# The fifth passes of two context products placed in 64 rows each, with the steps of an attention pipeline rearranged around them

## The chip, the cores and the metric

The kernel runs on one core of one Trainium2 chip. The metric is the device time of the whole kernel in microseconds (us). A difference under 0.2% of it, some 3 us, can't be told from no change.

## What is computed

```python
B, LQ, C = 32, 112, 256;  LKV, CTX = 375, 192;  H, DK = 16, 64      # for each of 32 batches:
q = layernorm(x) @ Wq;  k, v = split(ctx @ Wkv)                      # K = 192 rows of context
atten = softmax(q @ k.T * DK ** -0.5);  x = x + (atten @ v) @ Wproj + bproj
h = layernorm(x);  probs = softmax(h @ gate_w)                       # then 8 experts, the best 2 per token
x = x + sum over the 2 experts of share * (silu(h @ Wg) * (h @ Wu)) @ Wd
```

All in float32 accuracy. TensorE's products are made of parts: a matrix is split into a high part (`fp32r`) and a low rest, and high x high, high x low and low x high are added up in one bank.

## The kernel before

**Two stages.** From 35 us to about 1233 us of the profiled execution the attention of the 32 batches runs; then the rows are gathered per expert and 63 expert tiles follow. The change is in the first stage alone.

**A batch is four steps.** `pair(i)` does batches 2i (`odd` = 0) and 2i + 1, each in steps s = 0 to 3 of four heads. On TensorE (PE) a step is: scores of four heads into banks 0 to 3 (L1191); transposes of the softmaxed rows, `turn_prob`, two heads and then two (L1201); `weigh`, probabilities x V (L1220). Between them stand the products made ahead for the next batch: 8 products K (376 columns), 6 products V (512 columns), q (6 passes of 224 columns), xT. Which one stands where is the table `ahead(odd, s)` in three parts, `first`, `second`, `third`; all use banks 4 and 5 in turn (`Ahead.bank`, `bank_before`), and each waits until the bank's last content was copied out. In some steps stand also `turn_inverses` (step 1 and 3), `project` (step 0, the batch before), `turn_hn` (2), `gate_logits` (3) and `count` (1); these share bank 7 (`C_ps`).

**Row groups.** A head has 64 rows, so the score passes of two heads stand in rows 0 to 63 and 64 to 127 of the array and are issued as a pair. A context product (`product_ctx`, L1161) has 192 rows to sum over: passes 1 to 3 are the parts of the first 128; the other 64, the tail, take passes 4 and 5. Pass 4 multiplies the tail's weight `WkT` (the same 64 rows twice) by `yB`, whose upper 64 rows are the high part of the context and whose lower 64 its low part. Pass 5 multiplies the low part `WkU` by `yB`, 128 rows too.

**The other engines.** VectorE (DVE): the four row maxima of the scores (L973), the low parts of K and q (`low_part`, L851), two of four copies of transposed probabilities (L979), `normalise` (L903), `residual` (L911 to L918), routing (`choose`, `mark`, `assign`). ScalarE (ACT): the exponentials (L730), the high parts and V out of their banks (`evacuate`, L689 to L695), the other two copies (L736). GpSimd (POOL): the parts of the context (`split_y`), of the attention output (`split_O`), the norms and scatters. Each engine takes its instructions in the written order; semaphores carry all order between engines.

Of the kernel before, what the change touches and what calls it, by code (L numbers as in the profile page):

```python
# [32 lines left out]
P = 128  # L33
# [28 lines left out]

def ahead(odd, s):


    first = [("K", 2 * s), ("V", ((0, 2), (1, 0), (1, 2))[s]) if s < 3 else ("K", 7)]
    if odd:
        second = [("K", 2 * s + 1), ("q", s)] if s < 3 else [("q", s)]
    else:
        second = [("K", 2 * s + 1), ("q", HALF + s)] if s < 3 else [("xT", 0)]  # L70
    third = {0: [], 1: [("V", (1, 1))], 2: [("V", (0, 0))], 3: [("V", (0, 1))]}[s]
    if not odd:
        third = {2: [("q", 7)], 3: [("xT", 1)]}.get(s, []) + third
    return [(odd, s, part, kind, a) for part, items in enumerate((first, second, third)) for kind, a in items]


PAIR = [it for odd in (0, 1) for s in range(NS) for it in ahead(odd, s)]
assert len(PAIR) % 2 == 0 and [it[3] for it in PAIR[-2:]] == ["q", "V"]
START = [(1, -1, 0, kind, a) for kind, a in (
    ("K", 0), ("xT", 0), ("xT", 1), ("K", 1), ("K", 2), ("K", 3), ("q", 0), ("q", 1),  # L80
    ("K", 4), ("K", 5), ("q", 2), ("K", 6), ("K", 7), ("V", (0, 0)), ("q", 3), ("V", (0, 1)))]
START_BANKS = [k % 6 for k in range(len(START) - 2)] + [0, 1]
assert len(START) % 2 == 0
LAST = [it for it in PAIR if it[3] != "xT" and not (it[0] and (it[3] in "Kq" or it[4] in ((0, 0), (0, 1))))]


def n_split(items):
    return sum(it[3] != "V" for it in items)


class Ahead:


    def __init__(self, i):
# [3 lines left out]
        self.first = i is None  # L98
        self.n0 = base * len(START) + k * len(PAIR)
        self.split0 = base * n_split(START) + k * n_split(PAIR)  # L100
        self.v0 = base * (len(START) - n_split(START)) + k * (len(PAIR) - n_split(PAIR))
        self.bank0 = base * len(START) % 2

    def at(self, odd, step):

        return [[k for k, it in enumerate(self.items) if it[:3] == (odd, step, part)] for part in range(3)]
# [4 lines left out]
    def bank(self, k):  # L111
        return START_BANKS[k] if self.first else (self.bank0 + k) % 2

# [7 lines left out]
    def split(self, k):  # L121
        return self.split0 + n_split(self.items[:k + 1])
# [1284 lines left out]
```

## Time and profile before

| | us |
|---|---|
| median of 3 runs (1604.51 to 1605.93) | 1604.6 |
| profiled execution, its own time | 1601.43 |
| its span, first to last instruction | 1599.6 |
| PE busy / DVE busy / ACT busy | 1539.4 / 921.8 / 810.6 |

The granted clock of the core is 0.99 over the span. Rows of the profile name engine, line, operation and tile; `x12` is a count, `[0.58 <- ...]` idle time of the engine before the row and what ended it. A matmul's row lasts longer than its distance to the next one, since matmuls overlap: what one costs is read from the starts of neighbouring rows.

### The profile page before, as it was taken

The numbers are of one execution on the slowest core, as the hardware profiler recorded it, in microseconds if no ns is written. First come the engines' busy times: TensorE is split into PE (matmuls) and PEld (weight loads), VectorE is DVE, ScalarE is ACT, GpSimd is POOL, SyncE is SP. The second block draws the span as 40 slices with busy tenths as digits, with TensorE's granted clock in tenths as the row PEclk, the third lists the DMA queues.
The fourth block names the chain that finished last, engine by engine and source line by source line (L and its number), as shares of the span: only waits on it lengthen the run. The fifth ranks groups of instructions, "written<-read, shape, count | busy, mean of one in ns | idle before, by whom it ended". The sixth has DMA issues, their size and how long they took to land.

```text
span 1599.6 us, 37516 instructions
## 1 busy us (share of the span) xinstructions
PE 1539.4 (96%) x12134; PEld 1357.0 (85%) x12135; DVE 921.8 (58%) x2483; ACT 810.6 (51%) x2187; POOL 543.9 (34%) x603
## 2 busy tenths in 40 slices
PE   5999999999999999999999999999998599999997
PEld 4888888898889888898889888988887488888886
DVE  5566666666666666666666666666666633333332
ACT  4555555555556556555555555655554322222221
POOL 4224233433333233323342433333235223322332
PEclk9999999999999999999999999999999799999999
DMA  6411112111111112211111111112014333333332
GB/s 162 115 52 49 55 48 59 48 53 48 53 48 53 48 58 61 72 56 48 56 48 53 50 57 48 53 48 82 12 46 174 110 53 50 49 52 53 49 49 30
DMA packets 82704, 96.19 MB, mean 60 GB/s; under 512 B 6912, under 2 KB 77808, under 8 KB 82672
## 3 DMA queue, kind: packets, MB, share of 16 engines
q1 hardware_dynamic: 68960, 74.67, 16.1%
q0 software_dynamic: 12144, 15.66, 6.0%
q10 hardware_dynamic: 1568, 5.44, 1.0%
q8 instruction: 19, 0.31, 0.1%
q14 instruction: 13, 0.11, 0.0%
HBM read 44.85 MB, written 50.90 MB: 60 GB/s over the span
## 4 chain that ended last, share of the span: by engine, by line
PE 91%; DVE 3%; DMA 2%; ACT 2%; issue 2%; SPq 0%; POOLq 0%; DVEq 0%; ACTq 0%
PE bank L1161 30%; PE bank L1107 21%; PE bank L1220 10%; PE bank L1191 9%; PE bank L1201 9%; PE bank L1380 7%; PE bank L1364 2%; PE bank L1229 2%; PE bank L1324 1%; DMA WqL_whole<-in_L_xattn_Wq 1%; DVE probT L979 1%; PE bank L1270 1%; ACT K_h L691 1%; ACT prob L730 1%; DMA Wgu<-in_L_ffn_gate_up_w 0%
## 5 line engine op out<-in xcount | busy, mean ns | idle before, releaser
L730 ACT ACTIVATE prob<-bank,neg_max 112x375 f32<-112x375 f32 x512 | 295.0, 579 | 351.0 <-DVE neg_max L973 351.0
L973 DVE TENSOR_REDUCE neg_max<-bank 112x1 f32<-112x375 f32 x512 | 244.5, 540 | 77.5 <-PE bank L1191 75.6
L1201 PE MATMUL bank<-ident,prob 112*125 112x112 f32 x1536 | 212.7, 273 | 3.1 <-ACT prob L730 3.1
L1201 PEld LDWEIGHTS bank<-ident,prob 112*125 112x125 f32 x1536 | 198.7, 188 | 16.4 <-ACT prob L730 5.6
L851 DVE TENSOR_TENSOR K_l<-bank,K_h 128x376 fp32r<-128x376 f32 x256 | 140.2, 549 | 105.2 <-ACT K_h L691 104.4
L671 POOL DMA_INDIRECT out<-y_out,dest_now x63 | 97.8, 1552 | 244.4 <-ACT y_out L819 219.0
L1107 PE MATMUL bank<-Wgu,hT_h 128*128 x504 | 175.3, 429 | 2.7 <-DVE hT_l L1064 2.7
L1220 PE MATMUL bank<-probT,V 125*64 125x112 f32 x3072 | 175.5, 263 | 0.0
L596 POOL CAST OT_h<-O_now 128x448 fp32r<-128x448 f32 x64 | 35.7, 558 | 376.6 <-DVE O_now L903 376.6
L1220 PEld LDWEIGHTS bank<-probT,V 125*64 125x64 f32 x3072 | 148.0, 137 | 18.2 <-issue 0.4
L689 ACT COPY V<-bank 125x512 f32<-125x512 f32 x192 | 112.6, 586 | 93.8 <-PE bank L1161 89.4
L1085 DVE COPY hidT<-bank 128x512 f32<-128x512 f32 x63 | 43.5, 691 | 173.8 <-PE bank L1364 173.8
L691 ACT CAST K_h<-bank 128x376 fp32r<-128x376 f32 x256 | 120.6, 472 | 38.2 <-PE bank L1161 35.0
L979 DVE COPY probT<-bank 125x336 f32<-125x336 f32 x256 | 117.9, 501 | 31.8 <-PE bank L1201 31.7
L1161 PE MATMUL bank<-yA_h,WkH 128*128 128x376 f32 x256 | 109.5, 428 | 14.3 <-DVE WkU L869 14.3
L819 ACT ACTIVATE y_out<-bank,share_now 128x256 f32<-128x256 f32 x63 | 29.9, 475 | 179.3 <-PE bank L1380 179.3
L1380 PE MATMUL bank<-Wd,hidT 128*128 x504 | 119.1, 379 | 0.9 <-DVE hidT L1085 0.9
L1380 PEld LDWEIGHTS bank<-Wd,hidT 128*128 128x128 f32 x504 | 95.4, 189 | 16.4 <-issue 1.1
L903 DVE TENSOR_TENSOR O_now<-bank,inv_rows 128x448 f32<-128x448 f32 x64 | 40.0, 624 | 115.5 <-PE bank L1220 110.6
L1107 PEld LDWEIGHTS bank<-Wgu,hT_h 128*128 128x128 f32 x504 | 90.9, 191 | 18.1 <-issue 3.6
L730 ACT ACTIVATION_READ_ACCUMULATOR prob<-bank,neg_max 112x1 f32 x512 | 103.7, 203 | 0.0
L736 ACT COPY probT<-bank 125x336 f32<-125x336 f32 x256 | 101.5, 444 | 1.1 <-PE bank L1201 0.2
(163 smaller groups left out, 3676.5 us busy)
## 6 DMA issues: line engine op xcount, KB each, us to landing
bins<-pad_rows SPq DMA_DIRECT2D x29, 1032.0 KB, 6.2
h_in<-bins SPq DMA_DIRECT2D x63, 129.0 KB, 2.1
y_sb<-in_ctx SPq DMA_DIRECT2D x32, 187.5 KB, 2.4
y_sb<-in_ctx SPq DMA_DIRECT2D x62, 93.8 KB, 2.5
Wgu<-in_L_ffn_gate_up_w SPq DMA_DIRECT2D x4, 1024.0 KB, 5.0
Wgu<-in_L_ffn_gate_up_w ACTq DMA_DIRECT2D x4, 1024.0 KB, 9.8
x_sb<-in_x SPq DMA_DIRECT2D x16, 224.0 KB, 2.9
x_res<-in_x SPq DMA_DIRECT2D x32, 112.0 KB, 5.6
```

What stands on the lines that cost most here:

```text
L689: nc.scalar.copy(V[:, t, half * 512:half * 512 + 512], src[0:KR, :]).then_inc(v_done, 1)
L691: nc.scalar.copy(K_h[:, arg, :], src[:, 0:LKE]).then_inc(hi_done, 1)
L730: nc.scalar.activation(prob[:, j, :], S_ps[j][0:LQ, 0:LKV], ACT.Exp, bias=neg_max[:, j:j + 1], accum_out=row_sum[:, head // HB, head % HB: ...
L851: nc.vector.tensor_tensor(lo, ps, hi.bitcast(F32), ALU.subtract).then_inc(lo_done, 1)
L973: nc.vector.tensor_reduce(neg_max[:, j:j + 1], S_ps[j][0:LQ, 0:LKV], AX.X, ALU.max, negate=True).then_inc(max_done, 1)
L979: nc.vector.tensor_copy(probT[:, j, :], S_ps[j][0:KR, 0:KT * LQ]).then_inc(probT_first, 1)
L1107: last = mm(dst, w, m, start=n == 0, stop=n == len(todo) - 1)
L1161: last = mm(dst, w if weights_stay else y, y if weights_stay else w, start=n == 0, stop=n == len(todo) - 1)
L1191: last = mm(S_ps[2 * k + r][0:LQ, 0:LKE], w[rows, p, q], m[rows, p, :], start=n == 0, stop=n == len(todo) - 1)
L1201: last = nc.tensor.transpose(S_ps[j][0:KR, t * LQ:t * LQ + LQ], prob[:, j, t * KR:t * KR + KR], ident[0:LQ, 0:LQ])
L1220: last = mm(O_ps[r * DK:r * DK + DK, c:c + LQ], V[:, t, (2 * p + r) * DK:(2 * p + r) * DK + DK], probT[:, 2 * k + r, t * LQ:t * LQ + LQ], ...
L1380: last = mm(down_ps[(k + 1) % 2][:, 0:C], hidT[:, j, :], Wd[:, experts[k], j, :], start=j == 0, stop=j == FJ - 1)
```

## The change

1. Pass 5 of a context product now takes 64 rows, from a new tile `yT` (the tail's high part in both halves of the rows), and the fifth passes of two products are issued as a pair in the two row groups (`tails`). For the two K products of a step they come first, right behind the scores; for the two V products last, right behind `weigh` and ahead of the next step's scores. The start of the kernel keeps five passes.
2. Each step makes both its K products directly one after the other, and 2 V products in steps 0, 1 and 3 (none in 2). K and V use banks 4 and 5; q and xT use bank 7 except in step 2.
3. One V of each pair of V products is copied out by DVE (`SECOND`), the other by ACT as before.
4. The small work moves: `project` from step 0 to step 2, with `normalise` and `residual` accordingly; `turn_hn` to step 3; `gate_logits`, `choose`, `mark`, `count`, `assign` later too. DVE does the maxima first in each step.
5. POOL makes `yT` (one more cast per batch) and splits the context earlier in its order.
6. The start makes one more q and two more V products; the last batch makes two V fewer.

```diff
+    q_at = {(1, 0): (0,), (1, 1): (1,), (1, 2): (2, 3), (1, 3): (4,), (0, 0): (5,), (0, 1): (6,), (0, 2): (7,)}.get((odd, s), ())
+    one = [("q", p) for p in q_at] + {(0, 2): [("xT", 0)], (0, 3): [("xT", 1)]}.get((odd, s), [])
+    places = {"K": [("K", 2 * s), ("K", 2 * s + 1)],
+              "early": one if s < 2 else [],
+              "mid": one[:1] if s >= 2 else [],
+              "V": [("V", t) for t in {0: ((1, 1), (1, 2)), 1: ((0, 0), (0, 1)), 3: ((0, 2), (1, 0))}.get(s, ())],
+              "late": one[1:] if s >= 2 else []}
+SECOND = ((1, 2), (0, 1), (1, 0))
...
+                pool.tensor_copy(yT[:, slot, 0:LKV], y_sb[:, slot, 1, :]).then_inc(yT_done, 1)
...
+                    if arg in SECOND:
+                        dve.wait_ge(made, a.made(k))
+                        nc.vector.tensor_copy(V[:, t, half * 512:half * 512 + 512], src[0:KR, :]).then_inc(v_second, 1)
...
+            def tails(a, two, begin):
+
+                for r, k in enumerate(two):
+                    out, w, y = context_operands(a, k, 3, slice(r * CT, r * CT + CT))
+                    last = mm(out, w, y, start=begin, stop=not begin)
+                    if not begin:
+                        last.then_inc(made, 1)
...
                         if there(b, B):
                             scores(a, odd, s, b)
-                        for k in first[:1]:
+                        if of_K:
...
+                            for k in of_K:
+                                free_bank(a, k)
+                            tails(a, of_K, True)
+                            for k in of_K:
+                                context_product(a, k, False, True).then_inc(made, 1)
...
+                        if s == 2 and there(b - 1, B):
...
+                            project(b - 1)
                         if s == 3 and there(b - 1, B):
-                            gate_logits(b - 1)
...
+                            turn_hn(b - 1, 1 - odd)
                         if there(b, B):
                             turn_prob(b, s, 0)
-                        for k in second:
+                        for k in of_V[:1]:
+                            free_bank(a, k)
+                            context_product(a, k, True, False)
...
                         if there(b, B):
                             weigh(a, odd, s, b)
+                        if of_V:
+                            tails(a, of_V, False)
```

On PE, the end of step 0 and the start of step 1 before the change (`bank<-probT,V` is `weigh`, `K_h,q_h` and the like are scores, `yA_h,WkH` is pass 1 of a K product):

```order
L1220 MATMUL bank<-probT,V 64x112 [waits probT_first,v_done]
L1220 MATMUL bank<-probT,V 64x112 x5
L1220 MATMUL bank<-probT,V 64x112 [waits probT_second]
L1220 MATMUL bank<-probT,V 64x112 x5
L1191 MATMUL bank<-K_h,q_h 112x376 [waits lo_done]
L1191 MATMUL bank<-K_h,q_h 112x376
L1191 MATMUL bank<-K_l,q_h 112x376 x2
L1191 MATMUL bank<-K_h,q_l 112x376 x2
L1191 MATMUL bank<-K_h,q_h 112x376 x2
L1191 MATMUL bank<-K_l,q_h 112x376 x2
L1191 MATMUL bank<-K_h,q_l 112x376 x2
L1161 MATMUL bank<-yA_h,WkH 128x376 [waits lo_done]
```

The same place after it (L1281 is `weigh`, L1247 scores, L1219 `tails`, L1212 passes 1 to 4):

```order
L1281 MATMUL bank<-probT,V 64x112 x5
L1219 MATMUL bank<-WvU,yT 125x512 x2
L1247 MATMUL bank<-K_h,q_h 112x376 x2
L1247 MATMUL bank<-K_l,q_h 112x376 x2
L1247 MATMUL bank<-K_h,q_l 112x376 x2
L1247 MATMUL bank<-K_h,q_h 112x376 x2
L1247 MATMUL bank<-K_l,q_h 112x376 x2
L1247 MATMUL bank<-K_h,q_l 112x376 x2
L1219 MATMUL bank<-yT,WkU 128x376 [waits v_second,v_done]
L1219 MATMUL bank<-yT,WkU 128x376
L1212 MATMUL bank<-yA_h,WkH 128x376
L1212 MATMUL bank<-yA_l,WkH 128x376
```

The pair of V passes stands ahead of the scores and the pair of K passes behind them; the K pair waits for both copies of V out of banks 4 and 5, which nothing waited for at this place before.

On DVE, the end of step 1 and the start of step 2 after the change (L885 is the copy of V, L1017 the maxima, L895 the low parts of K, L947 `normalise`, L955 to L962 `residual`):

```order
L885 COPY V<-bank 125x512 [waits made]
L1016 REGISTER_ALU
L1017 TENSOR_REDUCE neg_max<-bank 112x1 [waits scores_made]
L1016 REGISTER_ALU
L1017 TENSOR_REDUCE neg_max<-bank 112x1 [waits scores_made]
```

The copy of V is new on this engine and stands ahead of all four maxima. Further on in step 2:

```order
L895 TENSOR_TENSOR K_l<-bank,K_h 128x376 [waits hi_done]
L944 ISA [waits inv_out]
L947 TENSOR_TENSOR O_now<-bank,inv_rows 128x448 [waits OT_lo,pv_made]
L954 REGISTER_ALU [waits xb_done,proj_made]
L955 TENSOR_TENSOR x_103<-bank,x_bias 112x256 [waits x2_out1]
L957 BN_STATS stat_106<-x_103 112x6 [waits x2_done]
L962 BN_AGGR mv_107<-stat_106 112x2 [waits st2,hn_twin]
L1023 COPY probT<-bank 125x336 [waits probT_made] x2
```

Before, `residual` stood ahead of the maxima of step 1:

```order
L911 TENSOR_TENSOR x_103<-bank,x_bias 112x256 [waits x2_out1]
L913 BN_STATS stat_106<-x_103 112x6 [waits x2_done]
L918 BN_AGGR mv_107<-stat_106 112x2 [waits st2,hn_twin]
L972 REGISTER_ALU
L973 TENSOR_REDUCE neg_max<-bank 112x1 [waits scores_made]
```

So `residual` now stands behind the maxima, and it is the copies of the transposed probabilities of step 2 that have it, and with it the wait for `project`, ahead of them.

## Rows read from the trace of the kernel before

**Rows 1.** The profile's first line: the span.
```profile
span 1599.6 us, 37516 instructions
```

**Rows 2.** Busy time by engine in one stretch: PE, PEld, DVE, ACT, POOL, granted clock, DMA.
```profile
500.00:1000.00 500.00, 497.42 (x4345) 444.71 (x4344) 319.81 (x892) 290.47 (x824) 175.00 (x215) 1.00 0.18 53
```

**Rows 3.** PE's waits in the whole span: us in total, times, longest.
```profile
PE bank L1161 <- DVE xT_l L851: 5.5, 15, 0.4
...
PE bank L1161 <- DVE WvU L869: 3.9, 1, 3.9
```

**Rows 4.** The chain that ended last, in order of time: start, us, what.
```profile
504.95 1.21 PE bank L1191 x12
...
529.80 2.81 PE bank L1107 x24
...
580.40 1.21 PE bank L1191 x12
```

**Rows 5.** Timeline of PE around the scores of one step: start, us, instruction.
```profile
505.66 0.33 PE L1191 MATMUL bank<-K_l,q_h 64*112 64x376 f32 x2
...
505.83 0.33 PE L1191 MATMUL bank<-K_h,q_l 64*112 64x376 f32 x2
...
506.09 0.44 PE L1161 MATMUL bank<-yA_h,WkH 128*128 128x376 f32 x1
...
506.37 0.33 PE L1161 MATMUL bank<-yA_l,WkH 128*128 128x376 f32 x1
...
506.54 0.33 PE L1161 MATMUL bank<-yA_h,WkL 128*128 128x376 f32 x1
```

**Rows 6.** The same step further on: V passes, transposes, the second K product.
```profile
507.98 0.39 PE L1161 MATMUL bank<-WvU,yB 128*125 128x512 f32 x1
...
508.21 0.81 PE L1201 MATMUL bank<-ident,prob 112*125 112x112 f32 x6
...
508.78 0.42 PE L1161 MATMUL bank<-yA_h,WkH 128*128 128x376 f32 x1
...
509.04 0.33 PE L1161 MATMUL bank<-yA_l,WkH 128*128 128x376 f32 x1
```

**Rows 7.** Timeline of PE in step 3 of the even batch.
```profile
519.71 0.35 PE L1129 MATMUL bank<-ident,xn 112*128 112x112 f32 x2
...
520.44 0.50 PE L1161 MATMUL bank<-WvH,yA_h 128*125 128x512 f32 x1 [0.37 <-DVE xT_l L851]
```

**Rows 8.** Timeline of DVE and ACT, step 3 (its first score pass starts at 514.56).
```profile
514.56 0.42 PE L1191 MATMUL bank<-K_h,q_h 64*112 64x376 f32 x2
...
515.36 1.91 DVE L973 TENSOR_REDUCE neg_max<-bank 112x1 f32<-112x375 f32 x4 [1.60 <-PE bank L1191]
...
515.95 0.57 ACT L730 ACTIVATE prob<-bank,neg_max 112x375 f32<-112x375 f32 x1 [2.19 <-DVE neg_max L973]
...
517.06 0.47 ACT L691 CAST K_h<-bank 128x376 fp32r<-128x376 f32 x1
```

**Rows 9.** Costliest groups: instructions by which DVE empties banks; mean ns of one.
```profile
L851 DVE TENSOR_TENSOR K_l<-bank,K_h 128x376 fp32r<-128x376 f32 x256 | 140.2, 549 | 105.2 <-ACT K_h L691 104.4
...
L1085 DVE COPY hidT<-bank 128x512 f32<-128x512 f32 x63 | 43.5, 691 | 173.8 <-PE bank L1364 173.8
...
L979 DVE COPY probT<-bank 125x336 f32<-125x336 f32 x256 | 117.9, 501 | 31.8 <-PE bank L1201 31.7
```

**Rows 10.** Timeline of DVE: `norm_x`; first and last of `mark`'s eight; `residual`.
```profile
511.27 0.74 DVE L832 BATCH_NORM_STATS2 stat<-x_sb 112x6 f32<-112x256 f32 x2
...
529.88 0.16 DVE L939 CAST top_f<-top_i 112x2 f32<-112x2 uint32 x1
...
530.57 0.16 DVE L954 TENSOR_SCALAR dest<-dest 112x2 f32<-112x2 f32 x1
...
532.65 0.42 DVE L911 TENSOR_TENSOR x<-bank,x_bias 112x256 f32<-112x256 f32 x1 [1.92 <-PE bank L1107]
...
533.72 0.18 DVE L918 BATCH_NORM_AGGREGATE mv<-stat 112x2 f32<-112x6 f32 x1 [0.18 <-DVE stat L913]
```

More of the change, by code:

```diff
@@ L55 @@
 W = C + 2
+PLACES = ("K", "early", "mid", "V", "late")
 def ahead(odd, s):
[L66 to L73, printed above, removed]
@@ new lines, with evacuated_as, how_many, bank_of @@
+LAST = [it for it in PAIR if it[3] != "xT" and not (it[0] and (it[3] in "Kq" or it[4] not in NOW))]
+def evacuated_as(it):
+    return "split" if it[3] != "V" else "values_y" if it[4] in SECOND else "values_x"
+def how_many(items, kind):
+    return sum(evacuated_as(it) == kind for it in items)
+def bank_of(items, k):
+    if items is START:
+        return START_BANKS[k]
+    odd, s, place, kind, a = items[k]
+    if kind == "K":
+        return a % 2
+    if kind == "V":
+        return int(a in SECOND)
+    return 7 if s != 2 else int(place == "late")
@@ L1007, in pair @@
                             turned(b, s, 1)
-                        if s == 1 and there(b - 2, B):
-                            assign(b - 2, odd)
-                        for k in second:
+                        for k in made_at["early"] + made_at["mid"]:
                             low_part(a, k)
@@ L1145, in make @@
                 else:
[L1146 to L1149 removed]
+                    assert a.first
+                    if kind == "V":
                         pe.wait_ge(w_lo, 5)
[L1151 to L1153 removed]
@@ L1155, in product_ctx @@
[L1155 to L1163 removed]
+                    elif arg == 0:
+                        pe.wait_ge(y_lo, 1)
+                        pe.wait_ge(yB_lo, 1)
@@ new lines, in make, with context_operands @@
+                    context_product(a, k, True, False)
+                    out, w, y = context_operands(a, k, 3)
+                    last = mm(out, w, y, start=False, stop=True)
+                last.then_inc(made, 1)
+            def context_operands(a, k, n, rows=slice(0, P)):
+                odd, step, place, kind, arg = a.items[k]
+                bank = START_ps[a.bank(k)]
+                slot = odd if kind == "V" and arg in NOW else 1 - odd
+                high, low, tail, tail_low = (WkH, WkL, WkT, WkU) if kind == "K" else (WvH, WvL, WvT, WvU)
+                w = {0: high, 1: high, 2: low, "both": tail, 3: tail_low}[n]
+                y = {0: yA_h, 1: yA_l, 2: yA_h, "both": yB, 3: yB if a.first else yT}[n]
+                if kind == "K":
+                    return bank[:, 0:LKE], w[rows, arg * P:arg * P + P], y[rows, slot, 0:LKE]
+                half, t = arg
+                return bank[0:KR, :], y[rows, slot, t * KR:t * KR + KR], w[rows, half * 512:half * 512 + 512]
@@ new lines, in context_product @@
+            def context_product(a, k, begins, ends):
+                for n in (0, 1, 2, "both"):
+                    out, w, y = context_operands(a, k, n)
+                    last = mm(out, w, y, start=begins and n == 0, stop=ends and n == "both")
+                return last
+            def tails(a, two, begin):
[4 more added lines that the diff above has]
+                        last.then_inc(made, 1)
```

297 lines of the change are left out of this document (162 added, 135 removed).

## Prediction

> **What bounds the kernel now.** I read the page first, then busy time by stretch, PE's waits, the chain in order of time, and the timeline of one pair of batches on every engine. The span is 1599.6 us [rows 1]; the time is counted from the profiled execution's own 1601.43 us, which lies 3.2 under the median of 1604.6, and that is added back at the end. In the steady part PE is busy 497.4 of 500 us while DVE has 320 and ACT 290 [rows 2]. A busy PE may still be one that waits inside overlapped rows, so the waits count more: over the whole span PE has one recurring wait, for the low part of xT, 15 times (once per pair of batches), and one of 3.9 us at the start for the low part of the V weights [rows 3]. In the chain the reader is to see the period: the scores that open a pair of batches start at 504.95 and again at 580.40, so **75.45 us per pair** [rows 4]. The kernel is bound by the number of passes that PE issues; what PE saves is saved in full, as long as no other engine becomes late.
>
> **What a pass costs.** It is the distance between two starts. Two score passes in the two row groups together take 0.17 us (505.66 to 505.83), and a full K pass of the same 376 columns takes 0.17 too (506.37 to 506.54) [rows 5]. A V pass of 512 columns takes 0.23 (507.98 to 508.21) [rows 6]. A change of kind costs about 0.09 more: from the last scores to the first K pass 0.26 (505.83 to 506.09) [rows 5], and the first fp32r pass behind transposes 0.26 (508.78 to 509.04) [rows 6].
>
> **The change, per pair of batches (16 K, 12 V products).**
> 1. *Fifth passes.* Now 16 x 0.17 + 12 x 0.23 = 5.5 us. As 8 + 6 pairs: for K the score pairs are the same operation in the same row groups with the same columns, so a pair takes 0.17. No pair of 512 columns is in the trace; it lies between one V pass, 0.23, and two, 0.46. I take 0.23, since the score pair shows no surcharge over one pass. Saving 8 x 0.17 + 6 x 0.23 = **2.74**; with V pairs at 0.46 it is 1.4, with both kinds unoverlapped 0.
> 2. *Both K products in a row.* The second K product has stood behind transposes; behind the first its first pass loses the 0.09: 8 x 0.09 = **0.7** saved. The V products all come behind transposes or small work; 4 of 12 stand directly behind a K product now and one behind q: 5 x 0.09 = **0.45** lost. `project`, 24 passes in 2.81 us [rows 4], no longer follows transposes: 0.2 saved. The tails need no change of kind of their own: the one from `weigh` to the scores is now paid by the V pair, the one from the scores to K by the K pair.
> 3. *xT.* Its two transposes take 0.73 us until the V product behind them starts (519.71 to 520.44), of which 0.37 is a wait for DVE's low part that has to free the bank [rows 7]; two transposes by themselves take 0.57 / 6 x 2 = 0.2 [rows 6]. In the new order no product in the same bank follows: **0.5** saved.
> 4. *Evacuation.* Six copies of V go to DVE. The nearest row, also 512 columns out of a bank, takes 0.69 us [rows 9]. POOL's extra cast hides in its idle 65% [rows 2].
>
> Sum on PE: 2.74 + 0.7 - 0.45 + 0.2 + 0.5 = 3.7 us per pair, if nothing waits.
>
> **What could be late.** The new waits are at two places.
> *K pair.* It follows the scores, 6 x 0.17 = 1.03 us after the step's start, and waits until both copies of V are out. The V pair ends about 0.17 after that start (starts 0.23 ahead, a V row lasts 0.39 [rows 6]). DVE's copy then runs from about 0.2 to 0.9, ACT's is no longer. Slack 0.1. Behind it on DVE are the maxima; they start 0.8 after the first score (514.56 to 515.36) [rows 8] since the scores are not there before. So the copy costs them at most 0.1. Queued behind the K pair on PE is everything of the step.
> *Transposes.* The first exponential starts 1.39 after the first score (514.56 to 515.95), two take 1.11, and the copy of K's high part 0.47 [rows 8]; it comes between them now. The second exponential, with its copy of K at 2.4 to 2.85 (K's first four passes end at 2.35), ends at about 3.4. PE reaches the first transposes of that head at 1.03 + 0.26 + 8 x 0.17 + 0.1 + `turn_hn` 0.3 + half the transposes 0.3 = 3.4 in step 3, later elsewhere: a tie. In steps 0 and 1 a q product stands ahead.
> *Step 2.* `project` starts 2.8 after the first score and takes 2.8: its result is there at 5.8. DVE's `residual` takes 532.65 to 533.90 = 1.25 [rows 10], then two copies of probabilities, 0.50 each [rows 9], together until 8.0. PE is at `weigh` at about 7.9 in the even batch (transposes, q, transposes, xT) and at 8.4 in the odd one, which has two q. It waits 0.1 to 0.2 once per pair.
> *DVE's fullest step* is step 1 of the even batch: V 0.69, maxima 1.91 [rows 8], two low parts of K 1.10, two copies 1.0, low q up to 0.55 [rows 9], `mark` 0.85, `norm_x` 0.74 and two aggregates of 0.18 [rows 10]: 7.2. The inverses and `choose`, seven instructions of 0.16 to 0.5 like the rows there, I put at 1.2. That is 8.4 in a step of some 8.8. It fits, barely. On the mean DVE goes from 320 of 500, 6.0 per step, to 6.5 per step of 9.0.
> I take 0.2 per pair for all of these: **3.5 us per pair**, new period 71.9.
>
> The Trainium skill bears on this twice. "TensorEngine Tiling (Array Packing)", section PSUM Bottleneck, says that packing speeds up TensorE but not the emptying of PSUM, which may then become the bottleneck. By that rule the time would go to rival B or D below instead of to the sum; with DVE at 320 of 500 us [rows 2] the trace leaves it room. "TensorE: Matmul & The Clock Gate", Part 3 (the cost: per-tile semaphore tail), gives 26 ns for every further increment of a semaphore by a tile. The V pairs carry one increment on each of their two passes; as an estimate by that page's figure this would add 6 x 0.026 = 0.16 us per pair of batches, 2.4 us in all. No row of before has such a pair of 512 columns.
>
> **Sum.** Pairs 0 to 14: 15 x 3.5 = 52.5. Batch 30: 4 x 0.17 + 3 x 0.23 + 4 x 0.09 = 1.7, and a q product (6 passes of 0.117, 2.81 / 24 [rows 4]) less: 2.4. Batch 31 makes two V products less, 2 x 1.2 = 2.4 of PE work, but without work to make ahead it is not bound by PE: I take 1 of it. The start makes those three products more; q fits in the 3.9 us wait [rows 3], two V products do not: 0 to 2.4 lost, I take 0.5, since the start also loses a q from among its V products. The end behind the last `weigh` keeps its chain. Together 55.4. 1601.43 - 55.4 = 1546.0, with the 3.2 of the median **1549**.
>
> **Rivals.**
> A. *As above*, at most 0.3 us more or less per pair: 1544 to 1555. Chance 0.64.
> B. *Partly given back to waits.* Speaks for it: the tie before the first transposes, slack of 0.1 at the K pair, 8.4 of 8.8 on DVE. Against: each is computed without a loss. If every step loses 0.15 us, 1.2 per pair, 15.5 pairs lose 18.6: 1568. Range 1555 to 1580. Chance 0.20.
> C. *Row-group pairs don't overlap for the context.* The score pairs speak against it. Without the 2.74: 15.5 x 2.74 = 42.5 less, 1591; with the V pairs alone at 0.46, 1.38 x 15.5 = 21 less: 1570. Chance 0.06.
> D. *Slower: DVE's copy of V comes late in all six steps that have one.* PE stands at the K pair with both row groups empty, while the maxima behind the copy are late too, so that the step shifts whole. It decides when the copies are late by more than 3.5 / 6 = 0.6 us each beyond the slack; 1 us late costs 6 - 3.5 = 2.5 per pair: 1604.6 + 15.5 x 2.5 = 1643. DVE's load of 73% and its written order, with nothing long between `assign` or `mark` and the copy except in one step, speak against. Chance 0.04.
> E. *More than that.* Batch 31 gains its full 2.4 and more, since the first steps of the last batch have less on PE, and waits hidden inside PE's overlapped rows go: 1537 to 1544. Chance 0.06.
>
> **Numbers.** A, E and the lower part of B with the lower part of C up to 1570 hold 0.8 and some: 1540 to 1571. Faster by over 0.2% (3.2 us, what a measurement can tell): all but D and a remnant of C, 0.95; within 0.2%: 0.01; slower: 0.04.
>
> **What would show it.** The chain should show the opening scores 71.5 to 72.3 us apart. The timeline: V pairs 0.23 to 0.25 and K pairs 0.17 apart from their neighbours, the second K product's first pass at 0.17, no wait for xT. PE's waits: a short one for DVE's `probT` in step 2 of even batches. If V pairs take 0.46, C; if PE waits for V, `v_second`, at the K pair or for `prob` at the transposes in every step, B or D. Wrong would also be a pass that got longer because two row groups read different tiles.

## The result, and the profile after

The changed kernel takes **1568.87 us** (median of 4 runs, 1568.5 to 1570.76) against 1604.82 before: ratio 0.9777, interval 0.976 to 0.9794. It is 36 us faster, where 55 were forecast: faster as predicted and inside the range of 1540 to 1571, but 20 us above the number and 14 above the range of the main forecast A (1544 to 1555), where rival B had been put (1568).

The first lines of the page of after, to be read beside [rows 1] and the table of before:

```profile
span 1566.4 us, 37570 instructions
...
PE 1503.0 (96%) x12134; PEld 1321.0 (84%) x12135; DVE 968.7 (62%) x2579; ACT 762.3 (49%) x2091; POOL 555.2 (35%) x636
```

The same 500 us as in [rows 2], busy time of PE, PEld, DVE, ACT and POOL:

```profile
500.00:1000.00 500.00, 499.71 (x4513) 444.84 (x4510) 350.81 (x963) 281.15 (x813) 182.36 (x234) 1.00 0.19 56
```

PE is now busy for all but 0.3 of the 500 us, and that row says nothing of waits: a matmul whose weights are loaded late overlaps the one before and hides the gap. So starts were compared. Where the span's 33.2 us come from, by the starts of the scores that open a pair of batches, the end of the last `weigh` and the start of the first expert tile in both traces:

| stretch | gain forecast | gain measured |
|---|---|---|
| start, until the first scores (35.79, after 38.97) | -0.5 | -3.2 |
| pairs 0 to 14 (period 75.45, after 72.63; first pair 71.95, after 70.25) | 52.5 | 41.3 |
| last two batches (68.7, after 68.8) | 3.4 | -0.1 |
| end of the last `weigh` until the experts (25.0, after 29.8) | 0 | -4.8 |

The span's miss is 22 of 55.4 (in the medians 20, since the profiled execution of before lay 3.2 under its median). Every term was too high, and the period accounts for only half of it. The timeline of after around the start of step 0 of an odd batch, and the same place one period later (start, us, instruction); it answers to [rows 5]:

```profile
507.96 0.49 PE L1219 MATMUL bank<-WvU,yT 64*125 64x512 f32 x2
...
508.29 0.33 PE L1247 MATMUL bank<-K_h,q_h 64*112 64x376 f32 x2
...
508.52 0.69 DVE L885 COPY V<-bank 125x512 f32<-125x512 f32 x1 [1.87 <-PE bank L1219]
...
509.14 0.33 PE L1247 MATMUL bank<-K_h,q_l 64*112 64x376 f32 x2
509.33 0.21 PEld L1219 LDWEIGHTS bank<-yT,WkU 64*128 64x128 f32 x2 [0.18 <-issue]
509.36 0.44 PE L1219 MATMUL bank<-yT,WkU 64*128 64x376 f32 x2
...
509.73 0.44 PE L1212 MATMUL bank<-yA_h,WkH 128*128 128x376 f32 x1
...
580.92 0.33 PE L1247 MATMUL bank<-K_h,q_h 64*112 64x376 f32 x2
```

The V pair costs 0.33 until the scores (508.29 - 507.96): 0.23 and a change of kind of 0.10, both as forecast. The last scores start at 509.14, so the K pair could start at 509.31 and its weights load ahead of it. They load at 509.33, just after DVE's copy of V has ended (508.52 + 0.69 = 509.21). The pair then needs 0.37 (509.36 to 509.73) until the first K pass. Step 3, where no V pair stands ahead and no copy has to be waited for:

```profile
536.70 0.19 PEld L1219 LDWEIGHTS bank<-yT,WkU 64*128 64x128 f32 x2
...
536.86 0.33 PE L1219 MATMUL bank<-yT,WkU 64*128 64x376 f32 x2
...
537.12 0.44 PE L1212 MATMUL bank<-yA_h,WkH 128*128 128x376 f32 x1
...
538.12 0.47 ACT L727 CAST K_h<-bank 128x376 fp32r<-128x376 f32 x1 [0.33 <-PE bank L1212]
...
538.49 0.58 ACT L767 ACTIVATE prob<-bank,neg_max 112x375 f32<-112x375 f32 x1
...
538.80 0.99 PE L1257 MATMUL bank<-ident,prob 112*125 112x112 f32 x6
...
539.56 0.48 PE L1212 MATMUL bank<-WvH,yA_h 128*125 128x512 f32 x1
```

Here the weights are loaded 0.16 ahead and pair to K pass is 0.26. So the late release would cost 0.15 per step (0.11 behind the pair, 0.04 ahead of it), six times per pair of batches; experiment 2 tests it. And the transposes (538.80) take 0.76 until the V pass, since the second exponential, behind the copy of K, ends at 539.07: six need 0.57 by [rows 6].

PE's waits in the whole span, to be read beside [rows 3]:

```profile
PE bank L1155 <- POOL OT_l L624: 7.2, 1, 7.2
PE bank L1155 <- DVE K_l L895: 4.0, 1, 4.0
...
PE bank L1290 <- DVE inv_wide L938: 2.4, 3, 1.6
PE bank L1257 <- ACT prob L767: 2.4, 3, 0.9
...
PE bank L1281 <- DVE probT L1023: 1.1, 2, 0.9
```

The 15 waits for xT are gone, as forecast. The rows that are left stand at three places: the start (K_l), the last two batches (inv_wide, prob, probT) and behind the last `weigh` (OT_l).

### The profile page after: what moved, and what is told of

The parts are those of the page before. It is cut to its first block and busy times, and to the rows that moved or that the text cites. A ratio compares the mean times of both kernels' runs of the same rounds, so it can differ in the third digit from the quotient of the medians.

```text
span 1566.4 us, 37570 instructions
## 1 busy us (share of the span) xinstructions
PE 1503.0 (96%) x12134; PEld 1321.0 (84%) x12135; DVE 968.7 (62%) x2579; ACT 762.3 (49%) x2091; POOL 555.2 (35%) x636
## 3 DMA queue, kind: packets, MB, share of 16 engines
q10 hardware_dynamic: 1568, 5.44, 1.0%
## 5 line engine op out<-in xcount | busy, mean ns | idle before, releaser
L1017 DVE TENSOR_REDUCE neg_max<-bank 112x1 f32<-112x375 f32 x512 | 243.9, 539 | 19.4 <-PE bank L1247 19.3
L895 DVE TENSOR_TENSOR K_l<-bank,K_h 128x376 fp32r<-128x376 f32 x256 | 140.4, 550 | 64.9 <-ACT K_h L727 62.4
L1281 PE MATMUL bank<-probT,V 125*64 125x112 f32 x3072 | 176.6, 264 | 2.0 <-DVE probT L1023 1.1
L1281 PEld LDWEIGHTS bank<-probT,V 125*64 125x64 f32 x3072 | 149.1, 137 | 14.6 <-issue 2.6
L885 DVE COPY V<-bank 125x512 f32<-125x512 f32 x96 | 66.4, 692 | 151.3 <-PE bank L1219 147.4
L725 ACT COPY V<-bank 125x512 f32<-125x512 f32 x96 | 56.4, 587 | 119.2 <-PE bank L1219 115.9
L1212 PE MATMUL bank<-yA_h,WkH 128*128 128x376 f32 x256 | 99.1, 387 | 14.5 <-DVE WkU L913 14.5
L673 POOL TENSOR_SCALAR std<-mv 112x1 f32<-112x1 f32 x32 | 7.7, 241 | 293.6 <-DVE mv L962 293.6
L767 ACT ACTIVATION_READ_ACCUMULATOR prob<-bank,neg_max 112x1 f32 x512 | 107.5, 210 | 0.0
```

Source lines behind the costliest of these rows:

```text
L767: nc.scalar.activation(prob[:, j, :], S_ps[j][0:LQ, 0:LKV], ACT.Exp, bias=neg_max[:, j:j + 1], accum_out=row_sum[:, head // HB, head % HB: ...
L895: nc.vector.tensor_tensor(lo, ps, hi.bitcast(F32), ALU.subtract).then_inc(lo_done, 1)
L1017: nc.vector.tensor_reduce(neg_max[:, j:j + 1], S_ps[j][0:LQ, 0:LKV], AX.X, ALU.max, negate=True).then_inc(max_done, 1)
L1212: last = mm(out, w, y, start=begins and n == 0, stop=ends and n == "both")
L1281: last = mm(O_ps[r * DK:r * DK + DK, c:c + LQ], V[:, t, (2 * p + r) * DK:(2 * p + r) * DK + DK], probT[:, 2 * k + r, t * LQ:t * LQ + LQ], ...
```

## Experiments

All diffs are against the changed kernel.

### 1. The pairing alone undone: `e1_single_tails`

```diff
-                y = {0: yA_h, 1: yA_l, 2: yA_h, "both": yB, 3: yB if a.first else yT}[n]
+                y = {0: yA_h, 1: yA_l, 2: yA_h, "both": yB, 3: yB}[n]
...
-                    out, w, y = context_operands(a, k, 3, slice(r * CT, r * CT + CT))
+                    out, w, y = context_operands(a, k, 3)
```

> The changed kernel with every fifth pass as before, alone in 128 rows, at its new place; all else stays rearranged. If a pair of passes in two row groups costs one pass, the period per pair of batches grows from 72.63 us by 8 x 0.17 + 6 x 0.23 = 2.74 to about 75.4, back to the 75.45 of before, and the time to about 1568.9 + 15.5 x 2.74 = 1611: the rearrangement alone would then be worth nothing in the steady part and lose at both ends. Rival: the pairs overlap only in part for 512 columns; then the period grows by 1.4 to 2 us, to 74.0 to 74.6.

Measured: 1613.72 (ratio to before 1.006, 1.0043 to 1.0077), period 75.6. The pairing is worth 2.97 per pair of batches; 2.74 was forecast. The other half of the result: the rearrangement by itself is no gain in the steady part (75.6 against 75.45). This run is 9.2 us slower than before (1604.54 beside it); its 15 pairs account for 3.5 of that by the starts, the rest lies in the ends.

### 2. Short copies of V: `e2_short_copies`

From the second pair of batches on both engines copy only 128 of the 512 columns of V, so three quarters of the later V are left out. On ACT, and alike on DVE:

```diff
-                    nc.scalar.copy(V[:, t, half * 512:half * 512 + 512], src[0:KR, :]).then_inc(v_done, 1)
+                    n = 512 if a.first or a.previous is START else 128
+                    nc.scalar.copy(V[:, t, half * 512:half * 512 + n], src[0:KR, 0:n]).then_inc(v_done, 1)
```

> The copies of V out of their banks take 128 of 512 columns from the second pair of batches on (the output is then wrong), so that both banks are free some 0.4 us earlier. Theory, late release: the K pair behind the scores starts late and without its weights loaded ahead since DVE's copy ends at 0.92 us of the step; then the distance from the K pair to the first K pass falls from 0.37 to 0.26 and that from the first scores to the pair from 1.07 to 1.03, six times, and the period from 72.63 to about 71.7, the time by some 13 us to 1555. Rival, fixed price: a pair whose weight load stands behind semaphore waits always costs this; then the period stays at 72.6.

Measured: 1558.14 (ratio 0.9716, 0.97 to 0.9732), period 71.7 to 71.95, against the expected 71.7 and 1555. The timeline of PE and of the copies at the same place:

```profile
504.92 0.33 PE L1249 MATMUL bank<-K_h,q_h 64*112 64x376 f32 x2
...
505.15 0.29 DVE L887 COPY V<-bank 125x128 f32<-125x128 f32 x1 [1.87 <-PE bank L1221]
...
505.95 0.34 PE L1221 MATMUL bank<-yT,WkU 64*128 64x376 f32 x2
506.21 0.44 PE L1214 MATMUL bank<-yA_h,WkH 128*128 128x376 f32 x1
...
576.70 0.33 PE L1249 MATMUL bank<-K_h,q_h 64*112 64x376 f32 x2
```

Scores to K pair is 1.03 instead of 1.07, K pair to K pass 0.26 instead of 0.37, as in step 3. What ended early is the copy; with the copy ending 0.5 ahead of the pair (505.44) instead of 0.1, both fall away. This is shown: the late release costs 0.8 per pair of batches, where six times 0.15 had been expected; the rival, a fixed price, would have left the period at 72.6.

### 3. Both exponentials ahead of both copies of K: `e5_two_exps_first`

```diff
                         if there(b, B):
                             weights_of(b, s, 0)
-                        for k in of_K[:1]:
-                            evacuate(a, k)
-                        if there(b, B):
                             weights_of(b, s, 1)
-                        for k in of_K[1:]:
+                        for k in of_K:
                             evacuate(a, k)
```

> ScalarE does the exponentials of the first two heads of a step before it copies the first K product, instead of one. Theory: in step 3 PE waits 0.18 us in the first transposes for the second exponential, which stands behind that copy and behind ScalarE's wait for the K product; the transposes of step 3 fall from 0.76 to 0.58, the period by 0.36 to 72.3, the time by 5.5 us to 1563. Rival: the copy of K is then 0.13 us later, VectorE's low part too, and the first V product waits for its bank instead: period 72.6.

Measured: 1563.92 (ratio 0.9747, 0.9731 to 0.9764), where 1563 was expected, most periods 72.23. PE in step 3:

```profile
538.37 0.36 PE L1314 MATMUL bank<-ident,hn 112*128 112x112 f32 x2
538.57 0.82 PE L1254 MATMUL bank<-ident,prob 112*125 112x112 f32 x6
539.15 0.48 PE L1209 MATMUL bank<-WvH,yA_h 128*125 128x512 f32 x1
```

The transposes take 0.58 again instead of 0.76. The wait for the second exponential is shown, 0.4 per pair with what follows from it, and the later copies of K cost nothing.

### 4. The V pair ahead of `weigh` in step 0: `e6_tails_first_s0`

```diff
+                        if of_V and s == 0:
+                            tails(a, of_V, False)
                         if there(b, B):
                             weigh(a, odd, s, b)
-                        if of_V:
+                        if of_V and s > 0:
                             tails(a, of_V, False)
```

> In step 0 alone the pair of V passes stands ahead of the weighing instead of behind it, so that V is copied out 1.3 us earlier; steps 1 and 3 stay. Late release: the K pair of step 1 costs 0.15 less, but the order transposes, V pair, weighing, scores has one change of kind more, 0.09 or more: per pair of batches 2 x (0.09 - 0.15), between 72.5 and 72.7. Fixed price: 2 x 0.09 more, 72.8.

Measured: 1570.16 (ratio 0.9787, 0.9771 to 0.9804), period 72.7 to 72.9. In step 1 the K pair no longer waits (pair to K pass 0.27), but there is a change of kind more: 0.43 from the V pair to `weigh`, where a V pass costs 0.23, and 0.26 instead of 0.17 from the first scores to the next. The period lies where the fixed price had been expected (72.8), not where the late release was (72.5 to 72.7): the release is no longer late, as the 0.27 shows, but the further change cost 0.20 and not the 0.09 that was taken. Moving the wait away this way costs what it saves.

### 5. GpSimd's split of expert 2 at another place: `e3a_expert2_early`, `e3b_expert2_last`

In POOL's order of the last batch it stands behind the norm that waits for `residual`, a `split_O` and a scatter. `residual` is two steps later now, and so the split starts at 1194.21, when the last `weigh` has begun (1193.50); before the change it started 11.6 us ahead of that `weigh` (1219.96 against 1231.54). Early:

```diff
                     if known(i) and i == NP - 1 and odd:
                         split_expert(1)
+                        split_expert(2)
...
-                    if known(i) and i == NP - 1 and odd:
-                        split_expert(2)
```

In the other it stands behind the last `split_O` instead.

> GpSimd splits expert 2 right behind expert 1 in the last batch, not behind the scatter of batch 29. Theory, queue: from the end of the last weighing to the first gathered row on PE it takes 29.8 us in the changed kernel and 25.0 before, since GpSimd's split of expert 2 (6.5 us, 1194.2 to 1200.7) stands ahead of the last split of the attention output, for which project waits 7.2 us. With it gone project starts 2.8 us behind the last weighing as before: 25 us. But GpSimd's long operation would now run under steps 1 and 2 of the last batch, where small VectorE operations have been stretched to its end: the last batch may take up to 4 us more than its 31.4. Total 1564 to 1568. Rival, the routing of batch 30 on VectorE sets the end, not GpSimd: no change of the 29.8.

> GpSimd splits expert 2 behind the last split of the attention output. Queue theory: project starts 2.8 us behind the last weighing; residual of batch 31 stands on VectorE behind the low part of expert 3, which waits for expert 2 (ready some 8.5 us behind the last weighing, plus 2.3), so that residual starts some 11 us behind it, against 12.3 in the changed kernel and 7.4 before: gain 1 to 2 us, 28 to 29 us in place of 29.8, time 1567.5. Rival: no change.

Measured: 1565.3 (ratio 0.9762, 0.9745 to 0.9778) and 1569.92 (0.9789, 0.9772 to 0.9805). The end of the last batch in the changed kernel, and the granted clock while `project` runs:

```profile
1193.50 1.37 PE L1281 MATMUL bank<-probT,V 125*64 125x112 f32 x24
1194.21 1.91 POOL L610 CAST Wgu<-Wgu 128x2048 fp32r<-128x2048 f32 x1
...
1196.21 4.50 POOL L604 TENSOR_TENSOR Wgu<-Wgu 128x2048 fp32r<-128x2048 f32 x1
1196.71 4.02 DVE L983 CAST top_f<-top_i 112x2 f32<-112x2 uint32 x1
...
1201.29 1.14 POOL L624 TENSOR_TENSOR OT_l<-O_now,OT_h 128x448 fp32r<-128x448 f32 x1
...
1202.57 0.53 PE L1155 MATMUL bank<-WpH,OT_h 128*112 128x256 f32 x1 [7.21 <-POOL OT_l L624]
...
1207.13 0.42 DVE L955 TENSOR_TENSOR x<-bank,x_bias 112x256 f32<-112x256 f32 x1 [2.35 <-PE bank L1155]
```

```profile
1202.00:1206.00 4.00, 3.43 (x17) 3.46 (x18) 2.78 (x4) 1.90 (x1) 0.43 (x1) 0.52 1.05 401
```

And with expert 2 early:

```profile
1198.25 0.34 PE L1154 MATMUL bank<-WpH,OT_h 128*112 128x256 f32 x1 [2.35 <-POOL OT_l L624]
...
1201.34 0.42 DVE L954 TENSOR_TENSOR x<-bank,x_bias 112x256 f32<-112x256 f32 x1
```

The last attention output waits behind 6.4 us of GpSimd's work; PE waits 7.2, and the clock is down to 0.52 (1.2 GHz) behind the wait, so that `project` itself takes 4.5 instead of 3.1. With the split early the wait is 2.35, the clock 1.00, and the end of the last `weigh` to the experts takes 23.5 instead of 29.8 (25 was expected). Before the change the wait there was 2.8, and `project` took 4.4 at a low clock too:

```profile
1236.00:1239.00 3.00, 3.00 (x17) 3.00 (x16) 2.11 (x1) 0.00 (x0) 0.00 (x0) 0.51 1.02 404
```

So of the 4.8 that the change lost in the tail, 4.4 are the longer wait (7.2 against 2.8), by one displaced instruction pair; the 1.4 of `project` come on top in the run with the split early. Its profiled execution was also the fastest of its four (1562.63); in the medians the gain is 3.6. With the split behind the last `split_O`, `project` no longer waits for it (2.35 again), but VectorE's last `residual` comes late and PE waits 6.2 for it: 29.0, and a total of 1569.92 against the expected 1567.5.

### 6. The fifth q later in the start: `e4_q4_later`

```diff
-    ("K", 6), ("K", 7), ("q", 3), ("q", 4), ("V", (0, 0)), ("V", (0, 1)), ("V", (0, 2)), ("V", (1, 0)))]
-START_BANKS = [k % 6 for k in range(len(START) - 4)] + [6, 7, 0, 1]
+    ("K", 6), ("K", 7), ("q", 3), ("V", (0, 0)), ("V", (0, 1)), ("q", 4), ("V", (0, 2)), ("V", (1, 0)))]
+START_BANKS = [k % 6 for k in range(len(START) - 5)] + [6, 7, 2, 0, 1]
```

> At the start the fifth q product stands behind two V products and not ahead of all of them. Theory: it waited 4.0 us for VectorE's low part of a K product, queued behind both low parts of the V weights, and held up the V products that were ready at 31.5 us; now the first V pass starts at 31.6 in place of 33.4 and the first scores at about 37 in place of 38.97: 2 us, 1567. Rival: V products wait for their own banks and copies and the first scores stay near 39.

Measured: 1568.95 (ratio 0.9785, 0.9768 to 0.9801), first scores at 38.45. The expected 2 us did not come: V now starts at 31.39, having waited 3.57 for the low part of WvU, and runs at a granted clock of 0.62. What was taken for the cause, q's place in the list, was only the first of two products behind the same late instruction. That led to the instruction itself, experiment 7.

This run's trace shows one thing more. Batch 31, the last, took 27.5 us here and 30.1 in the changed kernel, with the same instructions and the same kinds of wait. The granted clock differs. The row of 1175 to 1182, step 1 of that batch, of the changed kernel and of this run:

```profile
1175.00:1182.00 7.00, 6.39 (x44) 5.12 (x45) 3.33 (x16) 1.85 (x5) 0.81 (x1) 0.51 0.01 2
```

```profile
1175.00:1182.00 7.00, 6.21 (x66) 5.53 (x66) 4.81 (x19) 3.74 (x11) 0.94 (x1) 1.00 0.01 4
```

Before the change the clock was 1.00 over the whole batch. So 2.6 us of the changed kernel's last batch went with a clock at 1.2 GHz in the one execution that was profiled. What decides whether it falls there is not shown: PE had waited 0.94 us twice in the 12 us before, in this run as well, where it did not fall.

### 7. GpSimd's long operation behind VectorE's: `e8_wpl_later`

DVE and POOL at the start of the changed kernel:

```profile
24.58 1.45 DVE L913 TENSOR_TENSOR WvL<-WvL_whole,WvH 128x1024 fp32r<-128x1024 f32 x1 [0.57 <-ACT WvH L716]
25.96 5.56 DVE L913 TENSOR_TENSOR WvU<-WvU_whole,WvT 128x1024 fp32r<-128x1024 f32 x1
...
31.44 0.99 DVE L895 TENSOR_TENSOR K_l<-bank,K_h 128x376 fp32r<-128x376 f32 x2
```

```profile
25.03 5.40 POOL L649 TENSOR_TENSOR WpL<-WpL_whole,WpH 128x2048 fp32r<-128x2048 f32 x1
```

Two alike instructions take 1.45 and 5.56. The long one ends at 31.52, 1.09 after GpSimd's (30.43).

```diff
             pool.wait_ge(wp_done, 1)
+            pool.wait_ge(w_lo, 5)
             pool.tensor_tensor(wp_lo, wp[:].rearrange("p k n -> p (k n)"), wp_hi.bitcast(F32), ALU.subtract).then_inc(wp_done, 1)
```

> The changed kernel with one wait more: GpSimd makes the low part of the projection's weights (128x2048, 5.4 us, from 25.03 to 30.43 in the changed kernel) only when VectorE has made the low parts of the V weights. Theory S (VectorE's operations between two tiles in SBUF cannot run beside a long one of GpSimd): the low part of WvU, 5.56 us from 25.96 to 31.52 in the changed kernel, takes 1.2 to 1.5 like that of WvL ahead of it (1.45), and is done at 27.3; the low part of K behind it comes 4.2 earlier, q no longer waits 4.0, V products start at about 29.3 instead of 33.45 and the first scores at 34.8 to 35.5 instead of 38.97. Time 1565 (1564 to 1566) against 1568.9. Rival T (the 5.56 us are VectorE's own, by its operands, or come from ACT's casts at the same time): WvU still takes over 5 us and nothing moves, 1568 to 1570. Rival U (it takes 1.3, but the start then waits for something else, as in the run with q later): first scores 37 to 38.5, time 1567 to 1568.5.

Measured: 1562.59 (ratio 0.9746, 0.9729 to 0.9762). Its DVE and POOL:

```profile
25.73 1.21 DVE L914 TENSOR_TENSOR WvU<-WvU_whole,WvT 128x1024 fp32r<-128x1024 f32 x1
...
27.10 4.62 POOL L650 TENSOR_TENSOR WpL<-WpL_whole,WpH 128x2048 fp32r<-128x2048 f32 x1 [2.37 <-DVE WvU L914]
```

WvU takes 1.21, GpSimd's own operation 4.62 instead of 5.40, and the first scores come at 33.03 instead of 38.97. That is 5.9 earlier, more than the 4.35 that WvU lost (5.56 - 1.21): without its wait PE also keeps the clock. The row of a window over the V products, changed kernel and this one:

```profile
33.00:35.00 2.00, 2.00 (x8) 1.70 (x7) 1.33 (x4) 0.35 (x1) 0.00 (x0) 0.50 0.03 8
```

```profile
29.00:32.00 3.00, 3.00 (x15) 2.40 (x13) 1.36 (x4) 0.62 (x2) 2.72 (x1) 1.00 0.02 5
```

Theory S stands, with more than it expected (first scores 34.8 to 35.5, time 1564 to 1566). It goes further than the change: the 3.9 us wait of before for WvU's low part [rows 3] has the same form, there with WvL at 5.10 beside GpSimd's 4.59; that it has the same cause was not tested.

### 8. Expert 0's split out of the way of `inv_wide`: `e12_expert0_early`

In the last but one batch the changed kernel has

```profile
1158.51 2.64 DVE L938 COPY inv_wide<-inv_sum 112x512 f32<-112x512 f32 x1
```

```profile
1158.95 1.91 POOL L610 CAST Wgu<-Wgu 128x2048 fp32r<-128x2048 f32 x1
```

```diff
                     if not odd and (not known(i) or i + 1 < NP):
                         norm_x(i + 1)
+                    if known(i) and i == NP - 1 and not odd:
+                        split_expert(0)
...
-                    if known(i) and i == NP - 1 and not odd:
-                        split_expert(0)
```

> The changed kernel with GpSimd's split of expert 0 moved ahead within batch 30, from 1158.95 to about 1133.7, into a stretch in which GpSimd is idle and VectorE has only operations that read a bank. In the changed kernel the copy inv_wide (0.43 elsewhere) took 2.64 beside that split, 1158.51 to 1161.15, and PE waited 1.6 for it, out of 5.9 of waits in the last two batches (3.1 before the change). Theory S (operations between SBUF tiles are held by GpSimd's long ones): inv_wide takes 0.43 again, the last pair of batches gets 1.4 to 1.8 shorter, time 1567.3 (1566.5 to 1567.8) against 1568.9. Rival V (the split does the same to others where it now stands, or the exponentials set the last batch's pace anyway): no change, 1568.5 to 1569.5.

Measured: 1570.1 (ratio 0.9795, 0.9779 to 0.9812), against the expected 1567.3. The place itself did what was expected: `inv_wide` is

```profile
1161.67 0.43 DVE L938 COPY inv_wide<-inv_sum 112x512 f32<-112x512 f32 x1
```

PE no longer waits for it, and the last two batches take 67.2 instead of 68.8, all of it in the last but one (35.65 instead of 37.37). (In the changed kernel `inv_wide` begins 0.44 ahead of GpSimd's row; rows of that engine are rough in the profile. That the one held the other up is shown by the run, not by the rows.) But the first scores came 0.9 later, at 39.90, and from the third pair on the period was 72.74 to 72.87 instead of 72.63, about 2 us in all. In step 3 of the odd batch PE's inverses come 0.2 later than in the changed kernel, right after their input:

```profile
471.16 0.43 DVE L938 COPY inv_wide<-inv_sum 112x512 f32<-112x512 f32 x1
...
471.64 0.60 PE L1290 MATMUL bank<-ident,inv_wide 112*128 112x112 f32 x4
```

The instructions of the steady part are the same in both kernels, so this is a near tie there that falls one way or the other; what tips it was not found. The total fell where the rival (no change, 1568.5 to 1569.5) or worse had been expected; a gain of 1.6 us can't be read from a total here, only from its place.

### 9. The edits together: `e9_three_edits`, `e10_four_edits`, `e11_five_edits`

Edits 3, 5 (early) and 7; then with 6; then with 8.

> Three edits of the changed kernel together: both exponentials ahead of both copies of K's high part, the split of expert 2 right behind that of expert 1, and the wait at the start. If the three causes are separate their gains add up: 5.0 (alone, 1563.9) + 3.6 (alone, 1565.3) + 3.5 to 4 for the start = 12.4, 1556.5 (1555 to 1558). If they share a limit (the exponentials' order costs at the start, where the first scores came 1.5 later in that run, or the last batch takes the gain of the tail back), 1559 to 1562. A version that then beats both kernels by the edits that the profile names: before 1604.8, changed 1568.9.

> The three edits together and as a fourth the later place of the fifth q product in the start's list (alone it gave nothing, 1568.95: the low part of K was then late for the V products' bank too). If the start now waits for the V weights alone, the order of q and V makes no difference: within 1 us of the run with three edits. If q's place still counts, 1 to 2.5 faster, since the batch 31 took 2.6 less in the run with q later.

> The same move added to the four edits run together before (1554.04): 1552.5 (1551.9 to 1553.2) by theory S, 1553.7 to 1554.5 by rival V.

| | us, range | ratio to before, interval |
|---|---|---|
| three | 1555.58 (1554.87 to 1556.95) | 0.9703 (0.9686 to 0.9719) |
| four | 1554.04 (1553.63 to 1554.61) | 0.969 (0.9674 to 0.9706) |
| five | **1551.18** (1550.66 to 1552.11) | 0.9675 (0.9659 to 0.9691) |

The expected 1556.5 had counted 3.5 to 4 for the start, which then gave 6.3. The single gains are 5.0 + 3.6 + 6.3 = 14.8 and would make 1554.1; measured is 1555.58, 1.5 more. So they add up in the main, and the causes are separate as far as that shows; the last batch of the profiled execution took 31.9 instead of 30.1. With all five the kernel is 17.7 us faster than the changed one and 52.5 faster than before (1603.71 beside it; 1603.7 to 1604.5 beside all experiments). The fifth gained 2.9, more than its 1.6, and the time lies below the expected 1551.9 to 1553.2; the first scores of that run came 0.5 earlier by themselves. Four against three is a difference of 1.5 us, partly inside what single executions of the start vary by (first scores 33.2 and 34.5, the wrong way round); I leave it open whether q's place still counts.

## Why the prediction was right, and where its size was off

**Luck in the number.** The main forecast A, 1544 to 1555, is out. The time lies inside the stated range only because that was drawn up to 1571 for parts of B and C, and it lies 2 us inside that bound. All four terms erred to the same side, and none made up for another.

**Right.** That PE's passes set the period and that row-group pairs of 512 columns overlap fully: 0.33 for the V pair with its change of kind, K pairs at 0.17 and 0.26 where they don't wait. The term *Fifth passes*, 2.74, measured 2.97 by experiment 1. The second K product at 0.17 per pass, no wait for xT, a short wait for `probT` in step 2 of the even batch (0.1): as forecast. Rival C is out, though with the V pairs alone at 0.46 it had 1570, as near to the time as B: the pair's 0.33 and experiment 1 decide it. Rival D is out too, the K pair waits 0.15, far from the 0.6 at which it decides.

**The period, 71.9 forecast, 72.63 measured.** The mis-sized term is "I take 0.2 per pair for all of these" waits.
- *K pair, "slack 0.1"*. The copy does end 0.1 ahead of the pair, as worked out (508.52 to 509.21 against 509.31). The mistake was to take this for no wait: the weights of the pair are loaded ahead of it, and they too stand behind the semaphore. 0.8 per pair (experiment 2).
- *Transposes in step 3, "a tie"*. The tie falls on the wrong side by 0.18 in each of two batches: 0.4 per pair (experiment 3), where I had added nothing.
- *`project`, "0.2 saved"*. This one holds. By the starts it took 2.98 and 2.97 in the two batches before and takes 2.86 and 2.82 now; the 2.81 of [rows 4] is a row that begins 0.23 behind the first pass (529.57).
- The wait for `probT`, forecast 0.1 to 0.2, is 0.1.

Against these stands the 0.2 by which the pairing was worth more. From PE's sum of 3.7: 3.7 + 0.2 - 0.8 - 0.4 - 0.1 = 2.6, against 2.8 measured; 0.2 isn't assigned. (The 75.45 is right, though the scores at 504.95 and 580.40 don't open a pair of batches; they are those of step 2 of the even batch, a period apart.) The Trainium skill's rule from "TensorEngine Tiling (Array Packing)", PSUM Bottleneck, bears on the 0.8: no engine became full (DVE 351 of 500), but the emptying of two banks did become what the packed pair waits for. The estimate by "TensorE: Matmul & The Clock Gate", Part 3, of 0.16 per pair for the V pairs' increments does not show in the distance of the starts: 0.33 is 0.23 and the 0.10 that other changes of kind cost.

**The start, 0.5 forecast, 3.2 measured.** The step that failed is "q fits in the 3.9 us wait". PE now waits 4.0 for q and not for V: q's bank is released by the low part of a K product, which stands on VectorE behind the same late WvU. So q's six passes came behind the wait, at a granted clock of 0.50, and the first V pass 1.9 behind the end of WvU's low part (31.52 to 33.45) instead of 0.1 (30.87 to 31.01): 1.8 of the 3.2. The V products and the one q between the first V pass and the scores took 4.8 before, the four V products take 5.5: 0.7. The other 0.65 is WvU itself, which ends at 31.52 instead of 30.87. GpSimd's long operation beside it had moved 1.3 later (23.76 to 25.03), because the split of the next context was put ahead of it; the added cast of yT is 0.5 of that (21.80 to 22.30). The line "POOL's extra cast hides in its idle 65%" holds for the steady part and not here, and what stood in the way was more the split's new place than the cast. That GpSimd's operation makes the wait is shown (experiment 7); the three parts are read from the two traces.

**The last two batches, 3.4 forecast, 0.1 lost.** Of the 2.4 of batch 30, 0.1 came: PE waited 1.6 for `inv_wide` beside GpSimd's split of expert 0, shown by experiment 8. Of batch 31 "I take 1"; it took 0.2 longer (30.1 against 29.8), with the clock at 0.51 for 7 us of it. In the run with q later the same batch kept the clock and took 27.5 (experiment 6), so that these 2.6 hang on the execution and not on the order of the work; that is read from two traces, not from an edit. Without these two losses the term would have been above its forecast.

**The tail, "keeps its chain", 4.8 lost.** I looked at the chain on PE and not at what the move of `project` and `residual` does to POOL: the norm waits for it, and the split of expert 2 is queued behind the norm and ahead of the last `split_O` (experiment 5). Of a step that is moved every waiter counts, and this one was on the engine with 65% idle.

Rival B had the time right and the reason half: 0.15 per step at the K pair is its mechanism. As B took it, it costs 18.6 us; in the trace the period accounts for 11.2 of the span's miss of 22, and single events at the ends for the other 11. That its 1568 was met is luck in part.

## What to carry to other kernels

When a packed pair is put behind the emptying of its banks, ask for slack until its weights are loaded, not until its first pass starts; and where both exponentials are needed by the next work on PE, don't put a copy between them. In a kernel whose steady part repeats 15 times, the ends were still worth as much as the period: for each moved instruction follow its waiters on the idle engines too, and what is queued behind those. If two instructions of the same shape on VectorE take 1.2 and 5.6 us, look at what GpSimd does at that time. And before a change of some us at one place is put down to an edit, compare the granted clock of that place in both traces.

## What the runs showed of the hardware

**VectorE and GpSimd hold each other up.** Several of VectorE's instructions that read two tiles in SBUF, or copy or cast between tiles in SBUF, ended only after a long GpSimd instruction beside them. Before the change already, an instruction on 112 x 8 elements:

```profile
1207.09 4.60 POOL L578 TENSOR_TENSOR Wgu<-Wgu 128x2048 fp32r<-128x2048 f32 x1
...
1207.28 4.44 DVE L948 TENSOR_TENSOR chosen<-onehot 112x8 bf16<-112x8 f32 x1
```

4.44 us, until 1211.72, where GpSimd ends at 1211.69; in a batch of after with GpSimd idle it takes 0.17. Likewise top_f 4.02 and inv_wide 2.64 above. It works the other way too: GpSimd's WpL took 5.40 when WvL had started first (24.58 against 25.03), 4.62 when it came behind both; before the change, where it started first (23.76 against 24.33), it took 4.59 and WvL 5.10. Instructions that read a bank (the maxima, the low parts of K, V's copies) show no such stretch: V's copy took 0.69 throughout. This agrees with the Trainium skill, "SBUF — State Buffer", section "Who interferes with whom": the two engines share a pair of ports, whoever issues first has it for the whole instruction, and an instruction of VectorE with at most one input in SBUF outside its two-port modes isn't touched. `inv_wide` doesn't fit the order of issue by its rows, as said in experiment 8.

**The clock behind a wait.** PE waited 4.0 us at the start and 7.2 in the tail, and the granted clock was 0.50 and 0.52 (1.2 GHz) behind them; without the one and with the other down to 2.35 it was 1.00 (2.4 GHz) over the same work. So these waits cost more than themselves: 4.35 became 5.9 at the start, and `project` took 4.5 instead of 3.1. But behind the 2.8 of before it was 0.51 too, and in batch 31 it fell in one trace and not in another with the same waits of 0.94: the length of one wait doesn't settle it.

**A change of kind** costs about 0.1 at most places: V pair to scores 0.10 (0.33 against 0.23), K pair to full K pass and `weigh` to scores 0.09 (0.26 against 0.17). From a V pair to `weigh` it was 0.20 (0.43 against 0.23, experiment 4).
